# Three float32r products in place of one float32 product in the last pass of a four-layer attention stack, and a new order of all steps

## What is computed

```
# L3: q = x, k = v = context, N_HEAD = 16, D_K = D_V = 64, D_MODEL = 256
qh = (q @ w_q).reshape(B, Sq, N_HEAD, D_K).transpose(0, 2, 1, 3)      # w_q: 256 x 1024
kh = (k @ w_k).reshape(B, Sk, N_HEAD, D_K).transpose(0, 2, 1, 3)
vh = (v @ w_v).reshape(B, Sk, N_HEAD, D_V).transpose(0, 2, 1, 3)
scores = jnp.einsum('bhqd,bhkd->bhqk', qh, kh) / scale
attn = jax.nn.softmax(scores, axis=-1)
ctx = jnp.einsum('bhqk,bhkd->bhqd', attn, vh).transpose(0, 2, 1, 3).reshape(B, Sq, N_HEAD * D_V)
out = ctx @ w_fc + residual                                            # w_fc: 1024 x 256
out = (out - mean) * jax.lax.rsqrt(var + LN_EPS) * ln_gamma + ln_beta
```

## Time and profile before

| | |
|---|---|
| median of 3 runs | 4390.59 us (4389.6 to 4390.9) |
| span of the profiled execution | 4385.8 us |
| PE busy | 4260.8 us, 97% |
| PEld busy | 3436.5 us, 78% |
| DVE busy | 3663.2 us, 84% |
| ACT busy | 2547.7 us, 58% |
| POOL busy | 1590.0 us, 36% |
| mean granted clock of PE | 0.989 |

### The profile page before, as it was taken

One profiled execution on the slowest core, in us unless ns is written; L12 is line 12 of the kernel. 1 busy time (PEld: TensorE's weight loads), 2 busy tenths in 40 slices (PEclk: granted clock), 3 DMA queues, 4 the chain that ended last, 5 costly groups with the idle time before them and its releaser, 6 DMA issues. The chain is left out here.

```text
span 4385.8 us, 99261 instructions
## 1 busy us (share of the span) xinstructions
PE 4260.8 (97%) x33536; PEld 3436.5 (78%) x33536; DVE 3663.2 (84%) x12709; ACT 2547.7 (58%) x6753; POOL 1590.0 (36%) x2709
## 2 busy tenths in 40 slices
PE   5999999999999899999999999999999999999998
PEld 3788888888887677777777777778888888888886
DVE  4899999999997899999999999967777777777774
ACT  2556656566565545455454554536676767676765
POOL 3445454454452234444444444431222222222222
PEclk8999999999999999999999999999999999999999
DMA  5555455554553544545444454433222222222220
GB/s 172 147 154 161 133 151 153 140 161 138 149 157 114 152 132 137 141 127 163 133 146 132 133 149 124 135 98 84 62 78 61 79 61 79 61 77 63 72 66 9
DMA packets 406443, 513.40 MB, mean 117 GB/s; under 512 B 133808, under 2 KB 373936, under 8 KB 384432
## 3 DMA queue, kind: packets, MB, share of 16 engines
q1 hardware_dynamic: 398544, 496.82, 39.7%
q10 hardware_dynamic: 7392, 10.24, 0.7%
HBM read 266.30 MB, written 236.72 MB: 115 GB/s over the span
## 5 line engine op out<-in xcount | busy, mean ns | idle before, releaser
L816 ACT ACTIVATE probs_own<-bank 128x384 f32<-128x384 f32 (+2 forms) x1280 | 644.6, 569 | 80.0 <-DVE bank L1065 41.7
L723 ACT ACTIVATE ht<-bank,columns_l 128x256 f32<-128x256 f32 x384 | 197.2, 569 | 729.4 <-PE bank L1242 726.3
L625 POOL TENSOR_SCALAR veps<-meanvar 128x2 f32<-128x2 f32 x256 | 63.9, 249 | 1357.1 <-DVE meanvar L966 1357.1
L1189 PE MATMUL bank<-ht,w_ff 128*128 128x256 f32 x2048 | 489.8, 382 | 2.7 <-ACT ht L723 1.6
L1189 PE MATMUL bank<-w_ff,ffh 128*128 128x256 f32 x2048 | 475.7, 380 | 0.0
L1046 DVE DVE_READ_ACCUMULATOR2_ANT nmf_own<- 128x1 f32 x3072 | 433.5, 141 | 0.0
L1189 PEld LDWEIGHTS bank<-w_ff,ffh 128*128 128x128 f32 x2048 | 378.7, 190 | 49.4 <-issue 1.2
L1046 DVE CUSTOM_DVE_ANT_0 bank<-bank,mask_rows 128x256 f32<-128x256 f32 x1024 | 398.8, 457 | 21.2 <-PE bank L1189 21.1
L1189 PEld LDWEIGHTS bank<-ht,w_ff 128*128 128x128 f32 x2048 | 369.6, 190 | 50.0 <-ACT ht L723 2.8
L1189 PE MATMUL bank<-kstack_own,qstack_own 96*128 96x256 bf16 (+2 forms) x3072 | 370.1, 248 | 27.2 <-DMA kstack_own<-k_parts 18.7
L881 ACT ACTIVATE probs_other<-bank,negmax 128x120 f32<-128x120 f32 x1024 | 356.6, 383 | 59.6 <-DVE negmax L1169 59.6
(11 more groups left out here) (164 smaller groups left out, 10138.4 us busy)
## 6 DMA issues: line engine op xcount, KB each, us to landing
qstack_own<-q_parts SPq DMA_DIRECT2D x96, 768.0 KB, 5.7
kstack_own<-k_parts SPq DMA_DIRECT2D x64, 768.0 KB, 7.3
qstack_other<-q_parts SPq DMA_DIRECT2D x64, 768.0 KB, 5.9
q_parts<-q_parts_own SPq DMA_DIRECT2D x96, 384.0 KB, 2.5
q_parts<-q_parts_own SPq DMA_DIRECT2D x96, 256.0 KB, 2.3
k_parts<-k_parts_own SPq DMA_DIRECT2D x64, 384.0 KB, 2.9
q_parts<-other_parts SPq DMA_DIRECT2D x64, 384.0 KB, 2.5
other_words<-k_parts SPq DMA_DIRECT2D x64, 360.0 KB, 3.3
```

The source lines that it names most:

```text
L625: nc.gpsimd.tensor_scalar(veps[key][:, :], meanvar[key][:, :, 1], r["norms"][key]["eps"], None, ALU.add).then_inc(veps_ready.sem, 1)
L723: return nc.scalar.activation(out, in_, ACT.Identity, scale=scale, bias=bias)
L816: nc.scalar.activation(probs[key][0:rows, j % a.slots, 0:n], bank_of(u)[0:rows, 0:n], ACT.Exp, scale=a.scale).then_inc(a_done.sem, 1)
L1189: return nc.tensor.matmul(out, lhsT, rhs, start=first, stop=True, skip_group_check=True)
```

## The change

It does two things.

1. In the pass `l2` the products of `project_q3`, `project_v3` and `project_out3` are made of parts. Each operand x is split into `hi`, a copy of x to the type float32r (which rounds it), and `lo` = x - hi, also float32r. In place of x·w in float32 stand three float32r matmuls into the same bank, hi·hi, hi·lo and lo·hi (`mm3`). The keys' projection `project_k3` stays float32. The new steps that make the parts:
   - `norm` of `l2` on ACT writes `ht_hi` too, two more affine copies (128x256); `ht_lo` on POOL, two subtractions.
   - `context_hi` on ACT (128x240) and `context_lo` on POOL.
   - `probs_v3` on ACT writes `ot3_hi`; `rest3` on DVE makes `ot3_lo` out of the PSUM bank (128x512), four times an element; the bank is free only after it.
   - Once: `weights_hi` on ACT and `weights_lo` on POOL for `q3`, `v3` and `fc`.
   The parts lie in memory that the passes before use (`shared`): `ht_lo` in the masks' words, `ot3_lo` in `ffh`, `w_q3_hi` in `w_other`, and so on; `probs_t3` moves to the upper half of `kstack_own` and to `ctx_other`. Waits for the former users come with it.
2. `LISTS` is new for all three passes, `START` is 0, 32.35 and 65.44, and all corrections of `SPREAD` are zero.

The scratch for DMA descriptors also shrinks from 8192 to 512. The core of the diff:

```
-START = {"l0": 0.0, "l1": 33.12879, "l2": 66.18842}
+START = {"l0": 0.00000, "l1": 32.34766, "l2": 65.44362}
...
-            ff_out.ff.3/4.88122
+            ff_in.ff.2/5.04648 ff_in.ff.3/5.12784 ff_out.ff.0/5.26585 ff_out.ff.1/5.34026 ff_out.ff.2/5.49212 ff_out.ff.3/5.65859
...
-LAST_BY_DVE = {"project_q": "split_rest_q", "project_k": "split_rest_k"}
+LAST_BY_DVE = {"project_q": "split_rest_q", "project_k": "split_rest_k", "probs_v3": "rest3"}
...
+            elif kind == "context_lo":
...
+                nc.gpsimd.tensor_tensor(ct_lo[:, :, :], ct[:, u.element % 2], ct_hi[:, :, :].bitcast(F32), ALU.subtract).then_inc(
+                    context_lo_ready.sem, 1)
+            elif kind == "ht_lo":
...
+                for tag in w.latest_first(a_full, [("project_q3", "three", i) for i in range(4)], 1):
...
+                for f in range(FT):
+                    ins = nc.gpsimd.tensor_tensor(ht_lo[:, f, :], ht[key][:, f, :], ht_hi[:, f, :].bitcast(F32), ALU.subtract)
+                ins.then_inc(ht_lo_ready.sem, 1)
...
+                    if u.of == 2:
+                        affine(ht_hi[:, 0, :], bank[:, 0:T], gain[:, 0:1], shift[:, 0:1])
+                        affine(ht_hi[:, 1, :], bank[:, T:2 * T], gain[:, 1:2], shift[:, 1:2])
...
-                copy(ot3[:, 2 * j:2 * j + 2, :], halves(bank_of(u)[:, :])).then_inc(a_done.sem, 1)
+                if w.new(rest_ready, ("rest3", key, j), 1):
+                    act_e.wait_ge(rest_ready.sem, w.value(rest_ready, ("rest3", key, j), 1))
+                copy(ot3_hi[:, 2 * j:2 * j + 2, :], halves(bank_of(u)[:, :])).then_inc(a_done.sem, 1)
...
+            elif kind == "rest3":
...
+                bank = bank_of(u, ("probs_v3", key, j))[:, :].rearrange("p (f t) -> p f t", f=2)
+                v.tensor_tensor(ot3_lo[:, 2 * j:2 * j + 2, :], bank, ot3_hi[:, 2 * j:2 * j + 2, :].bitcast(F32), ALU.subtract).then_inc(
+                    rest_ready.sem, 1)
...
+        def mm3(out, lhsT, rhs, first):
+
+            mm(out, lhsT[0], rhs[0], first)
+            mm(out, lhsT[0], rhs[1], False)
+            return mm(out, lhsT[1], rhs[0], False)
...
+            elif kind == "project_q3":
+                split("q3")
+                hi, lo = r["three"]["q3"]
+                if w.new(ht_lo_ready, ("ht_lo", "1", 0)):
+                    pe.wait_ge(ht_lo_ready.sem, w.value(ht_lo_ready, ("ht_lo", "1", 0)))
+                bank = take(u)
+                for m in range(2):
+                    at = slice((2 * j + m) * P, (2 * j + m + 1) * P)
+                    for c in range(FT):
+                        ins = mm3(bank[:, m * T:(m + 1) * T], (hi[:, c, at], lo[:, c, at]), (ht_hi[:, c, :], ht_lo[:, c, :]), c == 0)
...
-                    ins = mm(bank[0:S2, :], x[:, c, :], wt[:, c, 512 * j:512 * j + 512], c == 0)
+                    ins = mm3(bank[0:S2, :], (ct_hi[:, c, :], ct_lo[:, c, :]), (hi[:, c, at], lo[:, c, at]), c == 0)
...
+                if w.new(rest_ready, ("rest3", "three", j)):
+                    pe.wait_ge(rest_ready.sem, w.value(rest_ready, ("rest3", "three", j)))
...
+                        ins = mm3(bank[:, t * C:(t + 1) * C], (ot3_hi[:, c, at], ot3_lo[:, c, at]), (hi[:, c, :], lo[:, c, :]), c == 0 and t == 0)
```

More of the change, by code:

```diff
@@ L125 @@
+            loads.rest.8/6.00000 loads.rest.9/6.25000 loads.rest.10/6.50000 store.x.0/6.55241 loads.rest.11/6.75000
+            loads.rest.12/7.00000
         """,
@@ L193 @@
+            nm_rows.other.0/3.44047 store.x.0/6.65390
         """,
@@ L523, in _ @@
             elif kind == "load_c":
-                for count, tag in passes[max(u.element - 2, 0) // NB]["ct_users"](a_full, d_full):
+                for count, tag in passes[max(u.element - 2, 0) // NB]["ct_users"](a_full, d_full, context_lo_ready):
                     if w.new(count, tag, 2):
@@ L749, in _ @@
                     act_e.wait_ge(a_full.sem, w.value(a_full, u.tag))
+                if u.of == 2 and kind == "norm":
+                    if first:
+                        reuse(act_e, w, u, xhat_ready, [("norm", "2", 0)], u.element - 1)
+                    if w.new(ht_lo_ready, ("ht_lo", key, 0), 1):
+                        act_e.wait_ge(ht_lo_ready.sem, w.value(ht_lo_ready, ("ht_lo", key, 0), 1))
                 for count, tag in ahead["ht_users"][key](a_full, d_full):
@@ L885, in _ @@
                 if first and j == r["first_of"]["turn3"]:
+                    reuse(act_e, w, u, a_full, [("scores_exp", "own", i) for i in range(16)], u.element - 1)
                     reuse(act_e, w, u, d_full, [("project_out", "other", 0)], u.element - 1)
@@ L1482, in sb, with shared @@
         return t[n]
+    def shared(*tensors):
+        for n, shape, dt in tensors[:-1]:
+            with nc.sbuf_tensor(n, shape, dt) as a:
+                t[n] = a
+        return sb(*tensors[-1])
     def each(keys, n, shape, dt=F32):
```

502 lines of the change are left out of this document (287 added, 215 removed), and 6 rows, old and new, of the table SPREAD.

## The result

The changed kernel takes **4783.4 us** (median of 4 runs, 4772.07 to 4789.04), the kernel before 4390.1 us beside it (4385.31 to 4390.9): a ratio of **1.089, with a 95% interval of 1.0877 to 1.091**. It is 393 us slower, where 141 us faster was forecast. The profiled execution has a span of 4770.3 us, 384.5 more than before.

A forecast was written before the change was run, and what follows sets the result against it. The prediction took PE, busy 97% and never waiting in the third pass, as the bound. Its terms, -137 + 5 - 15 - 4 + 4 + 6 = -141, took 4390.6 us to 4249 us, range 4208 to 4305.

The forecast's parts named there:

- 0.3% of the 2450 us of both: +6 us: First two passes: the new order inside them was to lose 0.3% of their time, +6 us.
- the new order is worse: Rival, first two passes: PE idles 2% of them and the border gives nothing, 4296 us; chance 0.15.
- -15 us: Border from first to second pass: a smaller planned distance was to save 15 us of idle time and low clock.
- -4 us: Start of the kernel: DVE's earlier work gives about 7 us back, the deeper plan takes some 3.
- +4 us: End of the kernel: the last element's chain is longer by affines, subtractions and rests, +4 us.
- -137 us: Third pass, PE: three float32r products at 0.110 us replace each float32 matmul, 4.3 us less per element.
- the rival of the weight loads: Third-pass products: weight loads are not hidden, +7.7 us per element, 4633 us; chance 0.05.
- that of float32 speed: Third-pass products: float32r runs like float32, +35 us per element, 5507 us; chance 0.02.
- the overlap rule: Products on PE: a cited page says LDWEIGHTS overlaps running matmuls only when the row group differs; bf16 rows of 0.110 us disagree.
- +5 us: Third pass: new links and DVE at 89% were to cost 0.4% of 32 x 40.0 us.
- The forecast's own warning: Third pass: an element above 41 us with PE below 98% says that a new link is not covered.
- its list of suspects: Third pass: PE's waits were to name an uncovered link as rest3, `ht_lo` or `ct_parts`.

The follow-up runs named there:

- experiment 4: Changed kernel with the 24 KB nm_rows.other transfer ahead of the two own stack transfers on SP in the first pass; 4678.7 us (one run).
- experiment 2: Kernel before with the new list of the first pass alone, second and third passes started 0.7 element later; 4699.1 us (one run).
- experiment 3: Kernel before with the float32r products and moved buffers, in the old order of all three passes; 4424.9 us, ratio 1.008.
- experiment 1: Changed kernel with the old lists, corrections and starts for the first and second pass; 4375.1 us, ratio 0.997.
- experiment 8: experiment 1 without rest3, the output projection taking ot3_hi a second time in place of ot3_lo; 4373.6 us, ratio 0.9966.
- experiment 11: experiment 1 with third-pass own maxima, negate.own and negate_t.own earlier on DVE, load_m and nm_rows.own ahead of spills on SP; 4318.7 us, ratio 0.983.

## Why the prediction was wrong

The steps as it put them:

- **"0.3% of the 2450 us of both: +6 us"** for the new order inside the first two passes. This is the step that failed first and most, and by itself turns the sign: 385 us were measured by the median elements (292 + 93). The reasoning was that PE idles only 10.7 of 2150 us there, "so there is little to win and more to lose", and that DVE at 92 to 94% is the danger. But a small idle time belongs to an order, not to the work, and says nothing of another order. The rival "the new order is worse" had the direction, with a size (2% idle, +32 us) more than ten times too small: idle was 13% in the first pass and 6% in the second. What it should have asked is on record in the lists: how far `nm_rows` stands from what SP issues before it (1.0 us behind 1.5 MB, experiment 4) and, for the `other` attention, from the scores behind it (0.11 element where there was 0.18).
- **"-15 us" for the border of the first two passes.** The planned distance did shrink: the second pass's first transposes come 31.05 median elements of the first pass behind its first value projection (47 us), instead of 31.88. But the second pass then takes 33.77 of its own median elements to the start of the third, where it took 32.95. What is won at the border, 0.83 x 51.05 = 42 us, is spent again, 40 us, nearly all in the second pass's first three slow elements. So the term is about zero, and it is not that nothing happened: the passes overlap more, and the overlap is slow. Those elements are as slow in experiment 4 (61, 57 and 60 us) and not in experiment 2 (48, 49 and 41), where the old second pass follows the new first. Whether the second pass's new list or its earlier start does it wasn't separated.
- **"-4 us" for the start** is not to be seen, and what there is points the other way: PE is busy for 82.1 of the first 150 us instead of 91.2.
- **"+4 us" for the end.** From the last element's first transposes to the end the old order takes 147.7 us, and with the products in it (experiment 3) 152.8: as forecast. In the new order of the third pass it takes 129.7, so there the term has the wrong sign. It is no net gain, since that order starts more slowly: in experiment 1 the second pass, itself unchanged, takes 15 us longer from its own first transposes to the third's (1512.6 and 1497.4 us).
- **"-137 us" for the products** (0.110 us each, 4.3 us an element). The mechanism holds: one float32r product costs about a quarter of a float32 one, so three for one gain, and neither the rival of the weight loads nor that of float32 speed came true. The size was off. A product takes 0.118 us and one of 512 columns 0.23, which makes 96 x 0.118 + 12 x 0.23 = 14.1 us, and the steps' starts add 0.9: 2.7 us an element saved, 86 in all. One half of the miss is the price of a product, whose low end was taken from bf16 rows as if nothing could lie between 0.110 and 0.43; the other half is the steps' starts, for which the sum had no term. As for the overlap rule that the prediction took from the Trainium skill, TensorE: Matmul & The Clock Gate (it stands there in the section The mechanism): products that start 0.118 us apart on the same 128 rows, with a weight load of 188 ns each, don't agree with it either.
- **"+5 us" for new links, since "PE never waits in the third pass".** This was the second failure: at 44.04 us an element, with 2.1 of them idle, the third pass gained 7 us by its median elements and not 132. The rests, whose cover it weighed, cost nothing (experiment 8). But the cover of a chain of fixed length is PE's work beside it, and that is what the change made shorter: beside the 11.4 us from queries to scores lie two steps of values and one of queries, 0.3 us less each. A PE that never waits says that its chains are covered now, not by how much. Experiment 3 points the same way for the old order (45.11 us, with waits of PE for the rows that the kernel before doesn't have); its chain was not followed. The forecast's own warning (above 41 us with PE below 98% "says that a new link is not covered") came true in its numbers, and its list of suspects did not.

With the loops open the products bring 2.1 us an element (experiment 11), 67 us, half of the forecast term; the rest of an element takes 27.2 instead of 26.6 us, and 0.3 of that is PE's wait for `probs_own`.

## What to carry to other kernels

When the bounding engine gets less to do, don't divide the saving into the pass: look for the chain that passes from one iteration into the next through in-order queues, add its fixed links to the engine's dense stretch, and see how far below the present period the sum lies. Such a chain can close through several queues at once, so a fix of one that gives nothing doesn't refute it; read which wait grew. And in a new order, look first at the smallest transfers that someone waits for, and at what stands directly ahead of them on their queue.

## What was not expected of the hardware

- A 24 KB transfer issued 1.0 us behind the second of two of 768 KB was there 7.9 us after its issue; issued 2.0 us behind the second of two stacks of 768 and 360 KB in experiment 4 (721.79 us) it was there after 4.9 (726.68). In experiment 11, with no stack ahead of it, it is issued at 3610.49, and DVE masks the scores that need it at 3613.93, so it was there within 3.4 us.
- A float32r product of 256 columns takes 0.118 us from start to start on 128 rows, with its own load of 128 four-byte weight columns recorded at 188 ns beside it. The Trainium skill, FP8 and Floating Point Precision, section TensorE Precision Notes, gives true float32 four passes through the array; the rows nearly agree, 0.43 us being 3.7 products of 0.118.
- Behind a wait of PE of 4.43 us the clock was at its lower level for 3.4 us. Between 400 and 1200 us of the changed kernel it is there 15 times, for 3.4 or 6.8 us each, about once an element, and the mean granted clock is 0.95. In experiment 4, where no wait in that stretch is longer than 3.4 us, it is there seven times, for 3.4 us each, and the mean is 0.99.
